# Beside L0's pass of a graph network kernel: part of the source order made by TensorE, edge rows in ten buffers, L3's score steps spread

## The chip, the cores and the metric

One core of one Trainium2 chip runs the whole program. The metric is the device time in microseconds, the median of several runs.

## What is computed

The reference chains four layers on 3125 nodes of 256 features and 50000 edges (`src`, `dst`, sorted by `dst` at the input but with padding and windows handled in the kernel):

```python
x = x + _L0_gnn_ref(_layernorm(x), edge_index, ...)   # sum over edges of h[src]*norm, by dst
x = x + _L0_ffn_ref(...)                              # shared expert and 2 of 8 experts
x = x + _L1_gnn_ref(_layernorm(x), edge_index, edge_attr_256, ...)  # relu(x[src] + edge_attr), by dst
x = x + _L1_ffn_ref(...)                              # 1 of 32 experts
x = x + _L2_gnn_ref(_layernorm(x), src, dst, ...)     # attention, softmax over edges of one src
x = x + _L2_ffn_ref(...)
x = x + _L3_gnn_ref(_layernorm(x), src, dst, ...)     # 4 heads, softmax over edges of one dst
x = x + _L3_ffn_ref(...)
```

The first, third and seventh line need the edges in the order of their target, the fifth also in the order of their source. The third needs the 50000 rows of `edge_attr_256` in the order of the targets.

## The kernel before, in words

The nodes are 25 tiles of 125 rows. Edges in order fill 415 tiles of 128 (`NTE`), none of which crosses a tile of nodes. Each of five engines runs its own program (VectorE `v`, ScalarE `a`, TensorE `p`, GpSimd `g`, SyncE `s`), stages are divided by `K.meet`, at which all five wait for one another, and inside a stage semaphores with counts (`mark`, `ring`) order the work. In the profile the engines are DVE, ACT, PE, POOL and SP.

**The sort** (`Sort`, L514 to L833) gives every edge a slot in the target order. Of the 391 columns of 128 edges, 56 are scattered by GpSimd through DRAM (`recd`, L831); the other 335 are moved by TensorE: VectorE makes a one-hot of the slot's row (L677) and one of its column (L680), ScalarE scales the first with the two halves of a 20-bit code (L795), and two products add them up in PSUM (L751). Meanwhile `EdgeRows` (L928 to L1026) starts to put the rows of `edge_attr` in order: SyncE loads 128 rows (L1008) into one of 5 buffers, GpSimd scatters them to the DRAM table `eaS` (L996), which frees the buffer. There are 391 such scatters, handed out in fixed numbers: 97 in the sort (`EDGES`, L518), 22 after L0's gathers, 2 and 3 (3 and 3 in odd steps) for each of the 25 steps of the stage with the shared expert (`fused_gpsimd`, L1482), and 2 or 3 for each of 54 expert tiles (`expert_gpsimd`, L1632). SyncE's loads are handed out in step with these.

**L0's pass** (`EdgeSum`, L1068 to L1141): for each of the 415 tiles GpSimd gathers 128 rows of `tabA` into a ring of 8 (L1086), VectorE makes a one-hot (L1105), TensorE multiplies (L1138, two instructions for one f32 product), and VectorE adds the result to the accumulator three steps later (L1117). `SourceSort` works beside it by steps of VectorE's loop: windows, picks (steps 30 to 54), scans (60 to 84), placing (120 to 169), and at step 180 the rows of the source order (`rowS`). `L0Out` (L1144) follows without a meet.

**The source order** is made by `SourceScatter` (L904): all 391 columns scattered into `recs` by GpSimd (L920), 2 for each of 54 expert tiles of the first mixture m0, 79 in `L1Mlp`, 2 for each of 25 steps of the scores of the second mixture m1, 19 in its grouping, 1 for each of its 54 expert tiles, and 3 for each of 25 steps of `L2Project` with 6 more after its loop. At its last tile of nodes SyncE waits for the scatters to land (L926), loads `recs`, and VectorE unpacks it behind its loop (L2358 to L2364).

**L3Sum** (L3192 to L3336) is a loop over the 415 edge tiles. TensorE picks scores for tile i-1 (L3322), and multiplies tile i-18 (L3331); VectorE makes the place one-hots of 8 tiles at once (`flip`, L3223), turns the picks of 8 tiles into scores in seven small steps in a row (L3263 to L3277, one group of 8 at a time), ScalarE takes their exponential (L3305), GpSimd weights the rows (L3244), and VectorE adds each product to the accumulator (L3284), each addition waiting for the one before it:

```python
            if i >= self.LAG + 2:
                k = i - self.LAG - 2
                rows = pr.acc[0:PT, bass.ds(at.at(k), AW)]
                v.wait_ge(*self.summed.n(k + 1))
                if k:
                    v.wait_ge(*self.added.n(k))
                v.tensor_tensor(rows, rows, K.bank[4 + k % 4][0:PT, 0:AW], ALU.add).then_inc(*self.added.up)
```

Of the kernel before, what the change touches and what calls it, by code (L numbers as in the profile page):

```python
# [17 lines left out]
N = 3125  # L18
D = 256
T = 25  # L20
# [62 lines left out]
class Kit:  # L83


    def __init__(self, nc, ctx, a, out):
# [23 lines left out]
        self.eidD = sb("eidD", [128, EP], I32)  # L110
        self.locD = sb("locD", [128, EP])
        self.idxS = sb("idxS", [128, EP], I32)
        self.locS = sb("locS", [128, EP])
        self.pkS = sb("pkS", [128, EC], I32)
        self.rowS = sb("rowS", [128, EC], I32)
        self.rowE = sb("rowE", [128, EC], I32)
# [4 lines left out]
        self.wiS = sb("wiS", [128, EP], I32)  # L121
        self.eaB = sb("eaB", [128, D])
# [391 lines left out]
class Sort:  # L514
# [6 lines left out]
    EDGES = 97  # L521
# [313 lines left out]
class SourceSort:  # L835


    def __init__(self, K, sort):
# [4 lines left out]
        self.of = K.W(EC)  # L843

# [6 lines left out]
    def vector(self, v, step):  # L851
# [40 lines left out]
        if step == 197:  # L892
            r.tile_windows(v, K.wtS).then_inc(*own.up)

    def tensor(self, p, step):
# [4 lines left out]
        if step == 193:  # L900
            self.rank.count_starts(p)


class SourceScatter:  # L904


    def __init__(self, K, sort):
        self.K, self.sort = K, sort
        self.sent = K.ring(4, EC, "gather", keep=True)
        self.done = 0  # L910

    def gpsimd(self, g, count):
        K = self.K
        if self.done == 0 and count:
            g.wait_ge(*self.sort.rows.n(1))
            g.wait_ge(*self.sort.ini_s.n(1))
        for c in range(self.done, min(self.done + count, EC)):
            if c >= 4:
                g.wait_ge(*self.sent.n(c - 4))
            g.indirect_dma_start(out=K.recs, out_offset=bass.IndirectOffsetOnAxis(ap=K.rowS[:, c:c + 1], axis=0),  # L920
                                 in_=K.pkS[:, c:c + 1], in_offset=None).then_inc(*self.sent.up(c))
            self.done = c + 1

    def landed(self, eng):
        for c in range(EC - 4, EC):
            eng.wait_ge(*self.sent.n(c))  # L926


class EdgeRows:
# [3 lines left out]
    NB = 5  # L933
    REST = 128 * EP

    def __init__(self, K, sort):
        self.K, self.sort = K, sort
        self.buf = [K.idxS[:, 0:D].bitcast(F32), K.locS[:, 0:D], K.wiS[:, 0:D].bitcast(F32), K.eaB[:, :], K.eidD[:, 0:D].bitcast(F32)]
# [126 lines left out]
class EdgeSum:  # L1065
# [31 lines left out]
    def vector(self, v):  # L1097
        K, acc = self.K, self.acc
        at = Offsets(K, ENG.DVE, K.wiD, 24 * 256)
        for i in range(1, NTE + self.LAG):  # L1100
# [17 lines left out]
            if self.beside:  # L1118
                self.beside.vector(v, i)
        v.wait_ge(*self.added.all)  # L1120

    def scalar(self, a):
        if self.edge_rows:
# [48 lines left out]
class Moe:  # L1172
# [289 lines left out]
    def fused_sync(self, s):  # L1462
# [7 lines left out]
        for t in range(T):  # L1470
# [6 lines left out]
            self.side.edges.sync(s, 6 if t % 2 else 5)  # L1477

    def fused_gpsimd(self, g):
        for t in range(T):  # L1480
# [5 lines left out]
            self.side.edges.gpsimd(g, 3 if t % 2 else 2)  # L1486
# [145 lines left out]
    def expert_gpsimd(self, g):  # L1632
        K = self.K
        for k in range(self.NT):
# [5 lines left out]
            if self.shared and k >= 2:  # L1640
# [3 lines left out]
                self.side.edges.gpsimd(g, k % 2)  # L1644
                self.side.source.gpsimd(g, 2)
# [604 lines left out]
class L2Project(Project):  # L2250
# [4 lines left out]
    def __init__(self, K, source):  # L2255
# [13 lines left out]
        self.raw, self.lo = W(EP, I32), W(EP, I32)  # L2269
        self.ptF = self.acc[:, 0:self.RT * DL]  # L2270
# [25 lines left out]
    def gpsimd(self, g):  # L2296
# [4 lines left out]
        self.source.gpsimd(g, EC)  # L2301

    def sync(self, s):
# [4 lines left out]
        for i in range(T + 3):  # L2308
# [7 lines left out]
            if i == T - 1:  # L2316
# [7 lines left out]
    def vector(self, v):  # L2324
# [33 lines left out]
        v.wait_ge(*self.got.n(1))  # L2358
        v.tensor_scalar(K.idxS[:, :], self.raw, 7, None, ALU.logical_shift_right)
# [832 lines left out]
class L3Sum:  # L3192


    GB, RO, RG, BUFS, LAG = 8, 24, 28, 4, 18
# [778 lines left out]
```

## Time and profile before

| | us |
|---|---|
| median of 3 runs | 5655.34 (5644.27 to 5657.37) |
| the profiled execution | 5645.28 |
| its span | 5643.2 |
| mean granted TensorE clock | 0.834 |

The profile is one execution, traced by the hardware; its span runs from the first instruction to the last. All times are in microseconds from the span's start, means of one instruction in ns. A bracket behind a row gives how long the engine sat idle before it and what ended that. A group's row ends with the idle time before its instructions. A granted clock (PEclk) of 1.00 is 2.4 GHz, one of 0.50 is 1.2 GHz; values between are mixtures over the window.

The stages that matter here lie at: sort 0 to 320, L0's pass 320 to 855, L0Out to 884, shared expert to 1089 and its meet to 1114, m0's experts to 1530, L1's pass from 1600 to 2150, L1Mlp to 2324, m1's scores to 2369 and their meet to 2391, m1's experts to 2600, L2Project 2645 to 2769, L3Sum 4985 to 5358.

### The profile page before, as it was taken

Reading aid. Unit: us, or ns where it says so; the run is one execution under the profiler, and the core shown is the slowest. Engines: PE = TensorE matmul, PEld = TensorE weight load, DVE = VectorE, ACT = ScalarE, POOL = GpSimd, SP = SyncE. Lnnn points to the kernel's source line nnn. Section 1 sums busy time; section 2 is a strip of 40 time slices with the busy share of each in tenths; the row PEclk is TensorE's granted clock in tenths of the full one; section 3 lists DMA queues with packets and bytes.
Section 4 is the critical chain, followed back from the end, with each engine's and each line's share of the span. In section 5 each row is a group of like instructions: output and inputs, shape, how many; then the busy total and the mean of one; then the engine's idle time right before and its main releaser. Section 6 shows DMA issues by size and latency. Waiting matters only on the chain. (4 is left out here: it accounts for less than half of the span.)

```text
span 5643.2 us, 86482 instructions
## 1 busy us (share of the span) xinstructions
PE 4436.4 (79%) x19744; PEld 2874.0 (51%) x19744; DVE 3377.0 (60%) x11730; ACT 2141.2 (38%) x7496; POOL 3551.8 (63%) x3818
## 2 busy tenths in 40 slices
PE   6968887799966778478599968888695788877768
PEld 4423336699823335344355546666593433345536
DVE  8957544310167774534455558887416688867775
ACT  7900002233333334112555545554243455544331
POOL 7777775677567773674777757775124477756620
PEclk8966658899957668555899989999696899999978
DMA  2543346688667771132344458886473588866500
GB/s 62 164 153 103 106 103 190 225 276 275 201 183 206 206 207 38 54 92 75 104 130 130 131 131 286 285 283 197 143 212 99 169 230 231 231 186 190 155 19 23
DMA packets 535499, 914.79 MB, mean 162 GB/s; under 512 B 103029, under 2 KB 385604, under 8 KB 526564
## 3 DMA queue, kind: packets, MB, share of 16 engines
q0 software_dynamic: 161600, 449.89, 28.5%
q1 hardware_dynamic: 312974, 330.74, 18.7%
q10 hardware_dynamic: 60438, 128.64, 7.4%
q8 instruction: 187, 3.06, 0.2%
q14 instruction: 300, 2.46, 0.1%
HBM read 739.18 MB, written 169.72 MB: 161 GB/s over the span
## 5 line engine op out<-in xcount | busy, mean ns | idle before, releaser
L1138 PE MATMUL bank<-small 128*125 128x256 f32 x1660 | 815.3, 611 | 298.6 <-DVE small L1105 175.4
L1086 POOL DMA_INDIRECT small<-tabA,idxD x830 | 801.6, 966 | 263.9 <-issue 189.5
L1138 PEld LDWEIGHTS bank<-small 128*125 128x125 f32 x1660 | 371.6, 276 | 741.6 <-DVE small L1105 401.3
L920 POOL DMA_INDIRECT recs<-pkS,rowS x391 | 385.6, 986 | 226.1 <-issue 100.7
L3085 POOL DMA_INDIRECT small<-tabC,idxD x415 | 410.6, 989 | 185.5 <-DVEq L204 59.4
L2823 POOL DMA_INDIRECT big<-tabB,idxD x415 | 399.4, 962 | 161.9 <-issue 90.5
L1117 DVE TENSOR_TENSOR big<-big,bank 125x256 f32 x830 | 346.4, 417 | 241.6 <-PE bank L1138 230.3
L2549 POOL DMA_INDIRECT big<-tabT,idxS x415 | 404.9, 976 | 136.4 <-issue 104.8
L1671 DVE COPY small<-bank 128x256 f32<-128x256 f32 x176 | 74.7, 425 | 679.4 <-PE bank L1726 679.4
L3163 PE MATMUL bank<-big,cst 128*125 128x512 f32 x830 | 426.1, 594 | 0.5 <-ACT big L3150 0.5
L1715 PE MATMUL bank<-small,big 128*128 128x128 f32 (+1 forms) x3040 | 399.2, 288 | 0.0
L1726 PE MATMUL bank<-big 128*128 (+1 forms) x1520 | 390.9, 404 | 2.4 <-issue 2.4
L1715 PEld LDWEIGHTS bank<-small,big 128*128 128x128 f32 (+1 forms) x3040 | 367.0, 195 | 19.3 <-issue 19.2
L3149 ACT ACTIVATE big<-cst,small 128x128 f32<-128x128 f32 x830 | 286.8, 393 | 235.3 <-DMA small<-tabC,idxD 233.5
L1639 POOL DMA_INDIRECT small<-tabA,small x176 | 169.0, 960 | 310.5 <-PE bank L1702 161.1
L3244 POOL TENSOR_TENSOR big<-big 128x256 f32<-128x256 f32 x415 | 245.5, 630 | 142.2 <-ACT big L3305 142.2
L3331 PE MATMUL bank<-big,small 128*125 128x260 f32 x830 | 268.4, 424 | 63.4 <-DVE big L3284 56.9
L1127 ACT ACTIVATE small<-small 128x256 f32<-128x256 f32 x415 | 172.8, 416 | 370.3 <-DVE small L1110 370.3
L1755 ACT ACTIVATE big<-bank,small 128x128 f32<-128x128 f32 (+1 forms) x760 | 220.7, 367 | 244.0 <-PE bank L1715 240.7
L1726 PEld LDWEIGHTS bank<-big 128*128 128x128 f32 (+1 forms) x1520 | 286.8, 199 | 51.4 <-issue 20.9
L2569 DVE SCALAR_TENSOR_TENSOR small<-bank,big 128x256 f32<-128x256 f32 x415 | 163.1, 421 | 220.2 <-PE bank L2647 219.8
L3132 DVE TENSOR_REDUCE small<-bank 125x4 f32<-125x512 f32 x415 | 282.2, 680 | 0.0
(521 smaller groups left out, 10439.8 us busy)
## 6 DMA issues: line engine op xcount, KB each, us to landing
big<-in_L_w ACTq DMA_DIRECT2D x56, 1024.0 KB
small<-eaS SPq DMA_DIRECT2D x415, 128.0 KB
eaS<-small SPq DMA_DIRECT2D x415, 128.0 KB, 3.8
big<-eaS SPq DMA_DIRECT2D x415, 128.0 KB, 2.8
big<-in_L2f_w ACTq DMA_DIRECT2D x64, 512.0 KB
big<-rowsD SPq DMA_DIRECT2D x104, 256.0 KB, 3.9
ytab<-small ACTq DMA_DIRECT2D x176, 128.0 KB
big<-rowsS SPq DMA_DIRECT2D x52, 256.0 KB
```

The costliest lines, as they stand in the source:

```text
L920: g.indirect_dma_start(out=K.recs, out_offset=bass.IndirectOffsetOnAxis(ap=K.rowS[:, c:c + 1], axis=0), in_=K.pkS[:, c:c + 1], in_offset=N ...
L1086: g.indirect_dma_start(out=self.gb[k % self.RG], out_offset=None, in_=K.tabA, in_offset=row_index(K.idxD, k)).then_inc(*self.got.up(k))
L1117: v.tensor_tensor(rows, rows, K.bank[k % 4][0:PT, 0:D], ALU.add).then_inc(*self.added.up)
L1138: p.matmul(self.K.bank[k % 4][0:PT, 0:D], self.oh[k % self.RO][:, 0:PT], self.gb[k % self.RG], start=True, stop=True).then_inc(*self.summe ...
L1715: m = p.matmul(self.hidden(k, hf)[0:hc, j * 128:j * 128 + 128], w1[:, c * F + f * 128:c * F + f * 128 + hc], xT[:, c, :], start=(c == 0), ...
L1726: m = p.matmul(K.bank[6 + k % 2][:, 0:D], self.hT[k % self.RT][0:hc, f * 128:(f + 1) * 128], K.big[0:hc, bass.ds(where + f * D, D)], start ...
L2549: g.indirect_dma_start(out=self.rows(k)[:, 0, :], out_offset=None, in_=K.tabT, in_offset=row_index(K.idxS, k)).then_inc(*self.got.up(k))
L2823: g.indirect_dma_start(out=self.gb[k % self.RB], out_offset=None, in_=K.tabB, in_offset=row_index(K.idxD, k)).then_inc(*self.got.up(k))
L3085: g.indirect_dma_start(out=self.gb[k % self.RG], out_offset=None, in_=K.tabC, in_offset=row_index(K.idxD, k)).then_inc(*self.got.up(k))
L3132: v.tensor_reduce(self.tm[k % 4][0:PT, 0:4], K.bank[k % L][0:PT, :].rearrange("p (h e) -> p h e", h=4), AXX, ALU.max).then_inc(*self.top.up)
L3149: a.activation(self.diagonals(k, h, 1), K.ident, ACT.Copy, scale=gb[:, D + h:D + h + 1])
L3163: p.matmul(b, K.ones[:, 0:PT], self.dg[k % self.RD], start=False, stop=True).then_inc(*self.field.up)
```

## The change

- The 10 edge buffers are one tensor `edge` (`NB = 10`); `idxS` and `locS` are views of it. Of the 391 edge scatters 80 (not 97) are in the sort, 28 (not 22) behind L0's gathers, 5 in each of the 25 shared-expert steps (not 5 or 6), 3 for each expert tile (not 2 or 3); SyncE's loads follow the same numbers.
- In the last 224 steps of L0's pass (191 to 414) a new class moves the first 224 source columns with TensorE as the sort does: two one-hots by VectorE, two scalings by ScalarE, two products by TensorE into banks 4 and 5. `total` folds them into `sumS` before L0Out (two VectorE operations), and L2Project adds `sumS` to `recs` (two more).
- GpSimd scatters only the other 167 source columns: 1 for each m0 expert tile (54), 79 in L1Mlp as before, 34 beside m1's experts, none in m1's scores and grouping, none in L2Project. `recs` is loaded at L2Project's third tile, not at its last.
- In L3Sum the seven score steps of a group go one at a time between additions, the exponential follows at a fixed step, and products lag by 24 tiles, not 18; `flip` and the place rows are asked for earlier or later to fit.

```diff
-    EDGES = 97
+    EDGES = 80
...
+class SourceMoves:
+    FIRST, N = 191, 224
+    RH, RP, RT = 4, 6, 6
...
+    def vector(self, v, step):
...
+        e = step - self.FIRST
+        if 0 <= e < self.N:
+            if e >= self.RH:
+                v.wait_ge(*self.scaled.n(e - self.RH + 1))
+            v.tensor_scalar(self.here[e % self.RH], self.iota16[:, 0:128], r.pf[:, e:e + 1], None, ALU.is_equal).then_inc(*self.here_v.up)
+            if e >= self.RT:
+                v.wait_ge(*self.placed.n(e - self.RT + 1))
+            v.tensor_scalar(self.ptile[e % self.RT], self.iota16, r.kk[:, e:e + 1], None, ALU.is_equal).then_inc(*self.place.up)
+
+    def scalar(self, a):
+        for e in range(self.N):
+            a.wait_ge(*self.here_v.n(e + 1))
+            if e >= self.RP:
+                a.wait_ge(*self.placed.n(e - self.RP + 1))
+            for b in range(2):
+                ins = a.activation(self.pl[e % self.RP][b], self.here[e % self.RH], ACT.Copy, scale=self.half[b][:, e:e + 1])
+            ins.then_inc(*self.scaled.up)
+
+    def tensor(self, p, k):
+        K, e = self.K, k - self.FIRST
+        if 0 <= e < self.N:
+            p.wait_ge(*self.place.n(e + 1))
+            p.wait_ge(*self.scaled.n(e + 1))
+            for b in range(2):
+                m = p.matmul(K.bank[4 + b][:, 0:EP], self.pl[e % self.RP][b], self.ptile[e % self.RT], start=(e == 0), stop=(e == self.N - 1))
+            m.then_inc(*self.placed.up)
...
-    NB = 5
+    NB = 10
...
-            self.side.edges.sync(s, 6 if t % 2 else 5)
+            self.side.edges.sync(s, 5)
...
-            self.side.edges.gpsimd(g, 3 if t % 2 else 2)
+            self.side.edges.gpsimd(g, 2)
...
-                self.side.edges.gpsimd(g, k % 2)
-                self.side.source.gpsimd(g, 2)
+                self.side.edges.gpsimd(g, 1)
+                self.side.source.gpsimd(g, 1)
...
-        self.source.gpsimd(g, EC)
+        assert self.source.done == EC
...
-            if i == T - 1:
+            if i == 2:
                 self.source.landed(s)
...
+        v.tensor_copy(self.rawf, self.raw).then_inc(*own.up)
+        v.wait_ge(*own.all)
+        v.tensor_tensor(self.raw, self.rawf, K.sumS[:, :], ALU.add).then_inc(*own.up)
...
-    GB, RO, RG, BUFS, LAG = 8, 24, 28, 4, 18
+    GB, RO, RG, BUFS, LAG, SCORE, EXP = 8, 30, 28, 4, 24, 11, 19
...
+            gi, r = divmod(i - self.SCORE, GB)
+            if 0 <= gi < self.n_g and r < 7:
+                self.score_step(v, gi, r)
...
-                 side=SideWork(edges, (0, 3, 0), source, (0, 2, 0)))
+                 side=SideWork(edges, (0, 3, 0), source, (0, 1, 0)))
...
-                 side=SideWork(None, None, source, (2, 1, 19)))
+                 side=SideWork(None, None, source, (0, 1, 0)))
...
-            edges.gpsimd(g, 22)
+            edges.gpsimd(g, 28)
```

`score_step(v, gi, r)` is the old block cut at its waits: r = 0 copies the picks out of PSUM, 1 and 2 add the two other parts, 3 to 6 form the score. `flip` moves from steps 0 to steps 2 of 8, so that its step has no score step.

## Rows read from the trace of the kernel before

**Rows 1.** Windows, core 0: us, busy of PE, PEld, DVE, ACT, POOL, PEclk, DMA share, GB/s

```profile
322.00:843.00 521.00, 421.73 (x823) 191.72 (x823) 316.18 (x952) 0.00 (x0) 395.38 (x412) 0.60 0.38 109
1160.00:1200.00 40.00, 40.00 (x277) 37.41 (x276) 6.46 (x30) 13.70 (x46) 30.33 (x32) 1.00 0.84 274
5014.00:5334.00 320.00, 246.13 (x1468) 173.62 (x1467) 237.64 (x735) 136.10 (x781) 217.31 (x368) 1.00 0.63 189
124.00:292.00 168.00, 159.40 (x804) 79.32 (x804) 166.18 (x764) 162.00 (x540) 131.86 (x117) 1.00 0.49 155
117.30:120.30 3.00, 2.94 (x9) 1.24 (x10) 2.96 (x16) 2.86 (x10) 2.18 (x2) 0.50 0.02 0
```

**Rows 2.** Timeline: VectorE's first work in L0's pass, GpSimd's last edge scatter before it

```profile
319.80 0.87 DVE L1105 TENSOR_SCALAR small<-cst,locD 128x125 f32<-128x125 f32 x3 [27.21 <-ACTq L204]
...
320.95 0.96 POOL L996 DMA_INDIRECT eaS<-locS,rowE  x1 [0.30 <-issue]
```

**Rows 3.** Groups of GpSimd, L0's pass, 600 to 840: busy, mean ns, idle before

```profile
L1086 POOL DMA_INDIRECT small<-tabA,idxD x193 | 182.5, 946 | 58.8 <-issue 47.2 <-PE bank L1138 11.6
```

**Rows 4.** Who VectorE waited for, shared expert's end: us, times, longest

```profile
DVE small L1663 <- issue: 25.4, 1, 25.4
```

**Rows 5.** Who VectorE waited for, m1's scores, then L2Project's end

```profile
DVE small L1398 <- SPq L202: 22.6, 1, 22.6
...
DVE idxS L2359 <- DMA big<-recs: 12.1, 1, 12.1
```

**Rows 6.** Groups of L3Sum, 5014 to 5334 us

```profile
L3284 DVE TENSOR_TENSOR big<-big,bank 125x260 f32 x367 | 155.4, 423 | 73.1 <-PE bank L3331 51.6 <-DVE big L3284 21.4
...
L3244 POOL TENSOR_TENSOR big<-big 128x256 f32<-128x256 f32 x368 | 218.3, 631 | 102.7 <-ACT big L3305 102.7
```

**Rows 7.** Groups of VectorE: the sort's one-hots (120 to 292), L0's addition (600 to 840)

```profile
L680 DVE TENSOR_SCALAR small<-big 128x416 f16<-128x416 f16 x328 | 104.0, 317 | 0.1
L677 DVE TENSOR_SCALAR small<-big 128x128 f16<-128x128 f16 x246 | 61.1, 248 | 0.0
...
L1117 DVE TENSOR_TENSOR big<-big,bank 125x256 f32 x191 | 80.5, 422 | 119.0 <-PE bank L1138 118.1
```

**Rows 8.** Timeline of TensorE: products back to back, one alone, moves at both clocks

```profile
343.74 5.90 PE L1138 MATMUL bank<-small 128*125 128x256 f32 x14
...
836.94 1.19 PE L1138 MATMUL bank<-small 128*125 128x256 f32 x2 [0.21 <-issue]
...
117.36 4.07 PE L751 MATMUL bank<-small 128*128 128x416 f16 x14 [0.88 <-ACT small L795]
...
139.87 1.68 PE L751 MATMUL bank<-small 128*128 128x416 f16 x8
```

**Rows 9.** Groups of GpSimd beside picks (362:392), scans (400:432), moves (185:290)

```profile
L1086 POOL DMA_INDIRECT small<-tabA,idxD x25 | 23.6, 946 | 7.6 <-issue 7.0 <-PE bank L1138 0.6
...
L1086 POOL DMA_INDIRECT small<-tabA,idxD x23 | 25.0, 1088 | 7.0 <-PE bank L1138 4.6 <-issue 2.4
...
L996 POOL DMA_INDIRECT eaS<-idxS,rowE x15 | 17.2, 1150 | 5.0 <-issue 4.3 <-DMA idxS<-in_ea 0.8
```

**Rows 10.** Timeline of GpSimd and VectorE, end of L0's pass and L0Out

```profile
856.15 1.20 POOL L996 DMA_INDIRECT eaS<-wiS,rowE  x1 [3.24 <-DMA wiS<-in_ea]
878.81 0.96 POOL L996 DMA_INDIRECT eaS<-eaB,rowE  x1 [0.30 <-issue]
...
883.26 0.30 DVE L1168 BATCH_NORM_AGGREGATE mv<-st 125x2 f32<-125x6 f32 x2
```

**Rows 11.** Timeline of VectorE inside L3Sum: score steps, additions, a flip

```profile
5101.65 0.22 DVE L3263 COPY small<-bank 128x64 f32<-128x64 f32 x1
5103.27 0.42 DVE L3284 TENSOR_TENSOR big<-big,bank 125x260 f32 x1
5103.89 0.42 DVE L3284 TENSOR_TENSOR big<-big,bank 125x260 f32 x1 [0.20 <-DVE big L3284]
5106.73 0.67 DVE L3223 TENSOR_SCALAR big<-big,lane 128x1024 bf16<-128x1024 bf16 x1
```

More of the change, by code:

```diff
@@ L893, in vector @@
             r.tile_windows(v, K.wtS).then_inc(*own.up)
+        self.moved.vector(v, step)
     def tensor(self, p, step):
@@ L908, in __init__ @@
         self.K, self.sort = K, sort
-        self.sent = K.ring(4, EC, "gather", keep=True)
-        self.done = 0
+        self.first = SourceMoves.N
+        self.sent = K.ring(4, EC - self.first, "gather", keep=True)
+        self.done = self.first
     def gpsimd(self, g, count):
         K = self.K
-        if self.done == 0 and count:
+        if self.done == self.first and count:
             g.wait_ge(*self.sort.rows.n(1))
@@ L917, in gpsimd @@
         for c in range(self.done, min(self.done + count, EC)):
-            if c >= 4:
-                g.wait_ge(*self.sent.n(c - 4))
+            n = c - self.first
+            if n >= 4:
+                g.wait_ge(*self.sent.n(n - 4))
             g.indirect_dma_start(out=K.recs, out_offset=bass.IndirectOffsetOnAxis(ap=K.rowS[:, c:c + 1], axis=0),
-                                 in_=K.pkS[:, c:c + 1], in_offset=None).then_inc(*self.sent.up(c))
+                                 in_=K.pkS[:, c:c + 1], in_offset=None).then_inc(*self.sent.up(n))
             self.done = c + 1
     def landed(self, eng):
-        for c in range(EC - 4, EC):
-            eng.wait_ge(*self.sent.n(c))
+        for n in range(EC - self.first - 4, EC - self.first):
+            eng.wait_ge(*self.sent.n(n))
 class EdgeRows:
-    NB = 5
+    NB = 10
     REST = 128 * EP
@@ L937, in __init__ @@
         self.K, self.sort = K, sort
-        self.buf = [K.idxS[:, 0:D].bitcast(F32), K.locS[:, 0:D], K.wiS[:, 0:D].bitcast(F32), K.eaB[:, :], K.eidD[:, 0:D].bitcast(F32)]
+        self.buf = [K.edge[:, i * D:(i + 1) * D] for i in range(self.NB)]
         self.rowE = K.rowE
@@ L1119, in vector @@
                 self.beside.vector(v, i)
+        if self.beside:
+            self.beside.moved.total(v)
         v.wait_ge(*self.added.all)
     def scalar(self, a):
+        if self.beside:
+            self.beside.scalar(a)
         if self.edge_rows:
@@ L2358, in vector @@
         v.wait_ge(*self.got.n(1))
+        v.wait_ge(*own.all)
+        v.tensor_copy(self.rawf, self.raw).then_inc(*own.up)
+        v.wait_ge(*own.all)
+        v.tensor_tensor(self.raw, self.rawf, K.sumS[:, :], ALU.add).then_inc(*own.up)
+        v.wait_ge(*own.all)
         v.tensor_scalar(K.idxS[:, :], self.raw, 7, None, ALU.logical_shift_right)
@@ L3226, in sync @@
         K = self.K
-        for q in range(3):
+        for q in range(4):
             self.places(s, q)
@@ L3232, in sync @@
             s.dma_start(self.gb[k % self.RG][:, 0:D], K.eaS[k * 128:(k + 1) * 128, :]).then_inc(*self.got.up(k))
-            if k >= 16 and k % 8 == 0 and k // 8 + 1 < self.n_g:
-                self.places(s, k // 8 + 1)
+            if k >= 8 and k % 8 == 0 and k // 8 + 3 < self.n_g:
+                self.places(s, k // 8 + 3)
     def inside(self, k):
@@ L3754, in _ @@
             K.meet(a, "a")
+            l0_sum.scalar(a)
             K.meet(a, "a")
@@ L3856, in _ @@
             edges.sync_last(s)
-            edges.sync(s, 5)
+            edges.sync(s, edges.NB)
             sort.sync_tables(s, edges)
@@ L3861, in _ @@
             l0_sum.sync(s)
-            edges.sync(s, 22)
+            edges.sync(s, 28)
             K.meet(s, "s")
```

105 lines of the change are left out of this document (70 added, 35 removed).

## The prediction

> **What bounds the kernel now.** I read the windows by stage first, then for each stage that the change touches what VectorE waited for at its end, and last the timelines inside the loops. No engine bounds the whole: each stage has its own limit, and an edit pays only where it shortens what ends a stage. The rows to look for are long waits at a meet, for there one engine holds four.
>
> The sort ends with such a wait. VectorE sat 27.2 us idle until 319.8, and GpSimd's last edge scatter is recorded at 320.95, each scatter taking 0.96 busy and 0.30 idle [rows 2] (GpSimd's records run a little behind its queue, so the meet precedes the last of them). L0's pass is paced by GpSimd's gathers: 0.946 + 0.305 = 1.25 us each, almost all the idle time "issue" [rows 3]; TensorE is busy for 422 of 521 us at a mean granted clock of 0.60, which leaves room in it [rows 1]. The shared expert's stage ends with VectorE waiting 25.4 us [rows 4] and GpSimd scattering all the while; m1's scores end with 22.6 us, L2Project with 12.1 us for `recs` [rows 5]. m0's experts are bound by TensorE: 40.00 of 40 us at full clock [rows 1]. In L3Sum VectorE has 51.6 us of waits for TensorE in 320, and TensorE itself is busy for 246 of 320 [rows 6, 1]: neither is full, because the seven score steps stand in a row in VectorE's queue.
>
> **The change part by part.**
>
> *Sort.* 17 scatters fewer before the meet, at 0.96 + 0.30 = 1.265 us: 21.5 us less. VectorE was done at 319.8 - 27.2 = 292.6 and the new meet would be at 298.3, so GpSimd still ends the stage and all 21.5 count: **-21.5**. At most 27.2 could be had; at least some 15, if the ten first loads crowd the stage.
>
> *Moves in L0's pass*, 224 steps. VectorE gets two one-hots, 0.317 + 0.248 us, beside an addition of 0.42 and a one-hot of about 0.3 [rows 7]: together 1.29 of busy time that overlaps at its edges, and less than 1.25 in pitch since the sort does one whole move in 176 us / 335 = 0.53 us with these same operations. ScalarE was idle here [rows 1] and has two scalings. TensorE: seven products back to back took 5.90 us, 0.84 each, at half clock; the pair of a move took 4.07 / 7 = 0.58, over a stretch that was at half clock for its first 3 us, and at full clock 1.68 / 4 = 0.42 at most [rows 8, 1]. At half clock a step wants about 0.84 + 0.69 = 1.53 (0.69 from twice 416 columns at 1.2 GHz), over the 1.25 of the gather; but then TensorE is always busy, and where it was so, 95%, with such moves (124 to 292) the clock was 1.00 throughout, as it was in L3Sum at 77% busy [rows 1]. At full clock the step wants about 0.42 + 0.42 = 0.84, and the gather stays the pace. What is left is what the new VectorE operations do to GpSimd. Beside 25 picks, 391 wide f16 comparisons, one per gather, a gather took 946 ns, as ever; beside the scans 1088; beside the sort's moves, a 416 wide comparison every 0.53 us, a scatter took 1150 [rows 9]. Bounds: nothing, and 0.19 x 224 = 43. The picks are the nearest row (same kind, same density), so I take little: **+5**.
>
> The Trainium skill (SBUF — State Buffer, Who interferes with whom) says that a comparison of this kind can take the port pair it shares with GpSimd, that the loser blocks until the instruction ends, and that this starves the descriptors of GpSimd's DMAs. The picks' 946 ns do not show it, the scans and moves may. It speaks against this change; as a mechanism of this kernel it is rival 2.
>
> *Between pass and shared expert.* `total` adds two VectorE operations on PSUM with their waits, about 1.3, to an L0Out that ended at 883.6. GpSimd has 28 scatters instead of 22: it ended at 879.8, with a stall of 3.2 for a load that ten full buffers avoid; 879.8 - 3.2 + 6 x 1.4 = 885.0 [rows 10]. Both end 1.5 later: **+1.5**.
>
> *Shared expert.* 125 scatters for 137, 12 x 1.27 = 15 us less, and the five loads of a step no longer wait for buffers. GpSimd needs 5 x 1.27 = 6.3 us per step of 198 / 25 = 7.9, so it should keep up and VectorE or TensorE end the stage. The whole wait is 25.4 [rows 4]; I take **-22**, bounds -15 and -25.4. Late next: the first gathers of m0's experts, unchanged.
>
> *m0's experts.* GpSimd issues 1 gather + 3 edges + 1 source per tile, 5 x 1.27 = 6.3 us, where it had 5.5 and 7.0; TensorE needs 40 / (277 / 50) = 7.2, at 50 instructions a tile, and covers it. Half an edge row more per tile is more traffic on DMA engines at 0.84 share [rows 1]; if the weights come late, that cover is gone. **+1**, bounds 0 and +8.
>
> *m1's scores.* GpSimd's 50 scatters (63 us) leave a stage whose other engines were done 22.6 us before the meet [rows 5]: **-22**. The 19 scatters of the grouping were hidden. L1Mlp is unchanged.
>
> *L2Project.* With no scatter to land, `recs` is there before the loop ends: -12.1 [rows 5], and +1.1 for the two added operations on 416 columns: **-11**. The loop itself waited for ScalarE and VectorE, not for GpSimd.
>
> *L3Sum.* A group of 8 tiles takes 320 / 367 x 8 = 6.98 us. From the first score step to the next addition VectorE spends 5103.27 - 5101.65 = 1.62, after 0.34 of the addition before; two additions with nothing between them stand 0.62 apart, since the second waits for the first (0.42 + 0.20) [rows 11]. A score step of about 0.2 fits into that gap. So a group loses 1.62 + 0.34 - 0.62 = 1.34, and gets 0.17 back at the flip, where now a step stands ahead of 0.5 to 0.67 [rows 11]: 1.17 x 52 = 61 less. The lag of 24 for 18 costs six short fill steps, 2 us. New pace 5.8 us per group; GpSimd needs 8 x 0.6 = 4.8 and TensorE 8 x 246 / 367 = 5.4 [rows 6, 1], so both are close but under it. **-59**, bounds -30 (TensorE or a hand-off takes over) and -80 (pace of TensorE, 5.4).
>
> *Sum*: -21.5 + 5 + 1.5 - 22 + 1 - 22 - 11 - 59 = **-128**. The profiled execution took 5645.3, 10 under the median of the three shown; from the median, 5655.3 - 128 = 5527.
>
> **The rivals.**
>
> 1. *Forecast*, 5527.
> 2. *GpSimd's gathers are slowed by VectorE's f16 one-hots.* For: scans and sort moves, +0.14 to +0.2 a piece [rows 9]. Against: the picks. 0.19 x 224 = 43, less the 5 counted: 5565.
> 3. *L3Sum finds another bound*: TensorE or the in-order queues, with a gain of 15 to 20 only. For: TensorE 77% busy with register loads in its stream. Against: additions 0.62 apart run in long rows. 5527 + 42 = 5569.
> 4. *TensorE falls behind in part of the moves*: at half clock 1.53 - 1.25 = 0.28, x 224 = 63: 5590.
> 5. *The other side: TensorE takes over L0's step.* It stays at half clock, and as it waits in order for one-hots, gather and scaled one-hots, nothing runs back to back: a product alone takes 1.19 [rows 8], then 0.15 to the next piece and 0.69 for the pair, 2.03 a step. (2.03 - 1.25) x 224 = +175 beside the other terms' -133: 5697, slower by 0.7%. It decides from 1.84 a step on. For: a mean clock of 0.60 in this pass. Against: the clock of 1.00 beside the sort's moves.
> 6. *More than forecast*: L3Sum at TensorE's pace, the whole 25.4 gained, no slowing of gathers: 5500.
> 7. *Not what it says*: late source data would have to be waited for elsewhere; the 167 scatters end in m1's experts, two stages ahead of their use, so this has nothing for it.
>
> **How the numbers follow.** Chances: forecast 0.58, 2: 0.13, 3: 0.11, 4: 0.06, 5: 0.04, 6: 0.08. 2 and 3 together would be 5607. The likeliest gives 5527. The range 5490 to 5592 takes in 6, 2, 3 and 4, with the bounds of the shared-expert and sort terms inside; 5 and pairs of rivals stay out. A measurement of this kernel tells about 0.3%, 17 us, from no change. Every case but 5 and double failures gives over 17 us: faster 0.93, same 0.03, slower 0.04.
>
> **What would show it.** Right: VectorE's idle time before L0's pass near 6 us and none over 5 at the shared expert's and m1's meets; gathers of L0's second half at a pitch of 1.25 to 1.30 with PEclk near 1.00 from step 191 on; in L2Project no wait for `recs`; L3Sum 310 to 316 us long instead of 373, additions 0.62 apart with one score step between. Wrong: gather pitch over 1.4; POOL waiting for PE in the pass; PEclk staying at 0.5 there; PE idle for weights in m0's experts; a group of L3Sum over 6.5 us.

## The result, and the profile after

The changed kernel takes 5519.4 us (5517.6 to 5524.2, 4 runs) against 5653.8 (5644.3 to 5657.4, 4 runs): a ratio of 0.9765, 95% interval 0.9752 to 0.9778, or 134 us less. 5527 was predicted, with a range of 5490 to 5592.

| | before | after |
|---|---|---|
| median | 5653.8 | 5519.4 |
| profiled execution, its span | 5645.28, 5643.2 | 5524.19, 5522.4 |
| mean granted TensorE clock | 0.834 | 0.853 |

The profiled executions differ by 121 us, not 134. Both traces can be laid beside each other instruction by instruction, as nearly every line exists in both; the table says by how much each stage became longer or shorter (the first or last instruction of a line in one trace against the same one in the other).

| stage | predicted | measured |
|---|---|---|
| sort, to L0's first addition | -21.5 | -23.7 |
| L0's pass, with 224 moves | +5 | +2.2 |
| `total` and what follows | +1.5 | +1.1 |
| shared expert with its meet | -22 | -22.6 |
| m0's experts | +1 | -2.7 |
| m1's scores with their meet | -22 | -22.5 |
| m1's experts | 0 | +1.7 |
| L2Project with `recs` | -11 | -11.1 |
| L2's combination loop (not changed) | 0 | +18.1 |
| L3Sum | -59 | -63.0 |
| all the rest | 0 | +1.7 |
| sum | -128 | -120.8 |

Without the loop that nobody had changed the stages add up to -139. A row of this table compares one execution with one, and the start of L0's pass alone moves by some us between executions (next paragraph).

**Sort** (the rows after to [rows 2]). The timeline of VectorE and GpSimd, then the same addition in the kernel before:

```profile
294.24 0.75 DVE L1175 TENSOR_SCALAR small<-cst,locD 128x125 f32<-128x125 f32 x3 [1.94 <-SPq L200]
306.14 0.42 DVE L1187 TENSOR_TENSOR big<-big,bank 125x256 f32 x1 [11.15 <-PE bank L1212]
...
297.80 0.96 POOL L1066 DMA_INDIRECT eaS<-edge,rowE  x1 [0.31 <-issue]
299.06 0.99 POOL L1156 DMA_INDIRECT small<-tabA,idxD  x1 [0.30 <-issue]
```

```profile
329.88 0.42 DVE L1117 TENSOR_TENSOR big<-big,bank 125x256 f32 x1 [9.20 <-PE bank L1138]
```

VectorE's wait at the meet is 1.9 us, not the 6 that were foretold, and yet the stage gained only 23.7. GpSimd's records run behind its queue: the meet opened at 294.2, while the last scatter is recorded at 297.80, and the rest of the wait moved behind the meet, to the first addition (11.15 for 9.20). The pair "wait at the meet, wait behind it" is to be read together. GpSimd's scatters run without a gap into its first gather, but the engine that VectorE's row names at the meet is now SyncE (`SPq`): the two end the stage close together.

Both numbers belong to this execution. Seven profiles below have this same sort (after twice, flip_gap, half_products, recs_late, short_weight, twice_onehot): VectorE waits 1.4 to 8.4 us at the meet, each time for SyncE, and the first addition starts at 305.1 to 311.0 us, at 308.2 in the mean. In the four profiles with the old sort it starts at 329.9 to 331.2, at 330.4 in the mean. Over all of them the sort gained 22 us.

**L0's pass and the other loops** (after to [rows 1]; windows: us, busy of PE, PEld, DVE, ACT, POOL, PEclk, DMA share, GB/s), and two groups of the pass between 560 and 800 (after to [rows 3, 7]):

```profile
560.00:800.00 240.00, 189.12 (x766) 94.70 (x767) 204.87 (x768) 132.76 (x383) 181.79 (x192) 1.00 0.37 106
4960.00:5220.00 260.00, 234.34 (x1467) 168.75 (x1467) 231.98 (x731) 140.94 (x780) 211.63 (x366) 1.00 0.77 229
1100.00:1140.00 40.00, 40.00 (x278) 37.41 (x277) 6.78 (x30) 13.74 (x46) 30.44 (x32) 1.00 0.95 310
```

```profile
L1156 POOL DMA_INDIRECT small<-tabA,idxD x192 | 182.4, 950 | 58.5 <-PE bank L1212 48.8 <-issue 9.7
...
L943 DVE TENSOR_SCALAR small<-small,big 128x416 f16<-128x416 f16 x192 | 65.6, 342 | 0.0
```

240 / 192 = 1.25 us per gather, 950 ns each: GpSimd still sets the pace and isn't held up. TensorE runs at full clock in the pass, where it had 0.60.

**The waits that should go** (after to [rows 4, 5]): what VectorE waited for behind the shared expert (us, times, longest), then its timeline across the meet behind m1's scores.

```profile
DVE small L1737 <- issue: 1.7, 2, 1.4
```

```profile
2322.86 0.18 DVE L1411 FIND_INDEX8 small<-small 125x8 uint32<-125x32 f32 x1
2323.18 0.18 DVE L1472 CAST small<-small 125x25 f32<-125x25 uint32 x1
```

25.4 us became 1.7. L1472 is the line that waited 22.6 us for the meet (L1398 before) and now follows the last index 0.14 us after its end; for `recs` VectorE doesn't wait at all any more (no such wait in 2640 to 2700).

**L3Sum** (after to [rows 6, 11]): groups of 4960 to 5220, then VectorE's timeline from a score step to a flip.

```profile
L3339 DVE TENSOR_TENSOR big<-big,bank 125x260 f32 x366 | 155.0, 423 | 28.0 <-DVE big L3339 8.7 <-PE bank L3422 3.1 <-issue 1.4
L3303 DVE TENSOR_SCALAR big<-big,lane 128x1024 bf16<-128x1024 bf16 x45 | 30.5, 677 | 0.0
L3367 DVE TENSOR_TENSOR small<-big,small 128x32 f32<-128x32 f32 x46 | 17.5, 380 | 0.0
L3370 DVE SCALAR_TENSOR_TENSOR small<-small 128x32 f32<-128x32 f32 x45 | 13.0, 289 | 0.0
L3373 DVE TENSOR_TENSOR small<-small 128x32 f32<-128x32 f32 x45 | 11.1, 246 | 0.0
...
L3359 DVE TENSOR_TENSOR small<-small,bank 128x64 f32<-128x64 f32 x46 | 9.8, 213 | 0.0
```

```profile
5050.21 0.42 DVE L3339 TENSOR_TENSOR big<-big,bank 125x260 f32 x1
5050.55 0.18 DVE L3373 TENSOR_TENSOR small<-small 128x32 f32<-128x32 f32 x1
5050.84 0.42 DVE L3339 TENSOR_TENSOR big<-big,bank 125x260 f32 x1
5051.18 0.17 DVE L3376 TENSOR_SCALAR small<-small 128x32 f32<-128x32 f32 x1
5051.26 0.48 DVE L3303 TENSOR_SCALAR big<-big,lane 128x1024 bf16<-128x1024 bf16 x1
5051.66 0.42 DVE L3339 TENSOR_TENSOR big<-big,bank 125x260 f32 x1
5052.28 0.43 DVE L3339 TENSOR_TENSOR big<-big,bank 125x260 f32 x1 [0.20 <-DVE big L3339]
```

Additions stand 0.63 apart (5050.21, 5050.84) with a step between them; only the flip stretches a gap, to 0.82. A group of 8 takes 260 / 366 x 8 = 5.68 us, where 5.8 was forecast, and VectorE's waits for TensorE fell from 51.6 us of 320 to 3.1 of 260. What was not foreseen: the three operations from L3367 on took 191 to 192 ns before and take 380, 289 and 246 now, and the flip 677 for 625. Those that read PSUM (L3359) did not become slower (213 for 220).

### The profile page after: what moved, and what is told of

It is laid out like the page before. It is cut to its first block and busy times, and to the rows that moved or that the text cites. A ratio compares the mean times of both kernels' runs of the same rounds, so it can differ in the third digit from the quotient of the medians.

```text
span 5522.4 us, 88485 instructions
## 1 busy us (share of the span) xinstructions
PE 4435.7 (80%) x20192; PEld 2884.0 (52%) x20192; DVE 3479.8 (63%) x12187; ACT 2302.5 (42%) x7944; POOL 3326.5 (60%) x3594
## 5 line engine op out<-in xcount | busy, mean ns | idle before, releaser
L1212 PE MATMUL bank<-small 128*125 128x256 f32 x1660 | 733.8, 555 | 286.9 <-DVE small L1175 172.2
L1212 PEld LDWEIGHTS bank<-small 128*125 128x125 f32 x1660 | 336.4, 251 | 680.7 <-issue 361.8
L2629 POOL DMA_INDIRECT big<-tabT,edge x415 | 404.0, 973 | 247.8 <-SPq L200 121.6
L1066 POOL DMA_INDIRECT eaS<-edge,rowE x391 | 393.0, 1005 | 164.7 <-issue 114.3
L951 ACT ACTIVATE small<-small,big 128x128 f16<-128x128 f16 x448 | 155.3, 394 | 385.3 <-DVE small L940 384.2
L2492 PE MATMUL bank<-big,small 125*128 x1245 | 217.1, 283 | 87.7 <-DVE small L2932 35.5
```

What stands on the lines that cost most here:

```text
L1066: g.indirect_dma_start(out=K.eaS, out_offset=bass.IndirectOffsetOnAxis(ap=self.rowE[:, c:c + 1], axis=0), in_=self.buf[c % self.NB], in_of ...
L1212: p.matmul(self.K.bank[k % 4][0:PT, 0:D], self.oh[k % self.RO][:, 0:PT], self.gb[k % self.RG], start=True, stop=True).then_inc(*self.summe ...
L2629: g.indirect_dma_start(out=self.rows(k)[:, 0, :], out_offset=None, in_=K.tabT, in_offset=row_index(K.idxS, k)).then_inc(*self.got.up(k))
```

## The experiments

Twelve kernels. For L3Sum "the loop" is the time from its first to its last addition (L3284, L3339 after) in the trace: 358.4 us before and 295.4 after. How far it moves by itself: nine profiles with after's L3Sum and a full weighting, the flip where after has it (after twice, edges76, five_buffers, half_products, l3sum_only, old_spread, recs_late, twice_onehot) have 293.3 to 297.2, 295.7 in the mean.

**1. L3Sum alone.** The class `L3Sum` of after in the kernel before; its diff is that of the change.

> The kernel before, with L3Sum of the kernel after and nothing else of the change. Theory (the parts are independent, each stage is paid for where its own end lies): the stages up to L2Project stay as they were and L3Sum's loop takes about 295 us instead of 358, so 5653.8 - 63 = 5591 us, ratio 0.989. Rival (the earlier stages' gains let later ones start in another state, or L3Sum gained only because GpSimd and the DMA engines had less left to do): L3Sum stays over 320 us, 5615 or more.

Measured: 5593.9 us, ratio 0.9887 (0.9863 to 0.9912), loop 295.6. The theory holds: L3Sum gains the same without the rest of the change, and this half is worth 0.0113 x 5655 = 64 us.

**2. The lag alone.**

```diff
-    GB, RO, RG, BUFS, LAG = 8, 24, 28, 4, 18
+    GB, RO, RG, BUFS, LAG = 8, 30, 28, 4, 24
```

> The kernel before, with only LAG 24 instead of 18 and RO 30 instead of 24 in L3Sum; the seven score steps still stand in a row. Theory (the gain comes from spreading the score steps, for the block costs VectorE 1.3 us per group of 8 in its own queue): the loop stays within 5 us of 358 plus the six extra fill steps, 5650 to 5658 us. Rival (the deeper lag is what hides the block's latency and brings most of the gain): the loop falls by 20 to 60 us, 5595 to 5635.

Measured: 5775.8 us, ratio 1.0208 (1.0182 to 1.0234), loop 470. Neither the theory nor the rival. VectorE's waits in L3Sum:

```profile
DVE big L3223 <- DMA big<-rowsD: 95.0, 41, 3.8
```

The place rows of a group were requested behind the load of row tile k, and that load waits for the product of tile k - 28: with a lag of 24 it comes six steps later, and the flip, which is due at a fixed step, stands ahead of the additions in VectorE's queue. The edit of SyncE's order in the change, to which the prediction gave no price, repairs this: it takes 97 of the 112 us away (experiment 3). Beside the 95 us of waits the granted clock was lower, too: at half for 174 us of this loop, for 5 in the kernel before.

**3. The lag with its row schedule.**

```diff
-    GB, RO, RG, BUFS, LAG = 8, 24, 28, 4, 18
+    GB, RO, RG, BUFS, LAG = 8, 30, 28, 4, 24
...
-        for q in range(3):
+        for q in range(4):
...
-            if k >= 16 and k % 8 == 0 and k // 8 + 1 < self.n_g:
-                self.places(s, k // 8 + 1)
+            if k >= 8 and k % 8 == 0 and k // 8 + 3 < self.n_g:
+                self.places(s, k // 8 + 3)
```

> The kernel before, with LAG 24 and RO 30 as in the run before this one and now also the place rows asked for as the change asks for them (four ahead, then row group k // 8 + 3 behind load k); the seven score steps still stand in a row. In the run before, VectorE waited 95 us for those rows. Theory (spreading the score steps is what gains; the lag alone gains next to nothing, and its row schedule only repairs what the lag breaks): L3Sum's loop 350 to 362 us, 5647 to 5660 us. Rival (lag and rows are most of the gain, the block in a row hardly matters once the pipeline is deep): the loop 300 to 320 us, 5595 to 5615.

Measured: 5672.0 us, ratio 1.0026 (1.0015 to 1.0037), loop 373.8. The rows no longer wait, but the loop is 15 us longer than before. A group and a window (5030 to 5330):

```profile
L3331 PE MATMUL bank<-big,small 128*125 128x260 f32 x653 | 240.5, 477 | 53.7 <-POOL big L3244 48.6 <-DVE big L3284 4.0
```

```profile
5030.00:5330.00 300.00, 244.93 (x1305) 173.33 (x1305) 213.64 (x653) 122.54 (x690) 190.26 (x327) 0.87 0.61 179
```

TensorE now waits for GpSimd's weighted rows where it waited for VectorE's additions, but it doesn't wait longer: over the whole loop it sat idle for 68 us, and for 80 in the kernel before. What grew is its own work, 306 us busy for 278, at a granted clock of 0.88 for 0.99: in this loop the clock fell to half 21 times, for 92 us together; before it fell once, for 5 us. A product took 473 ns for 423. It is not one bad execution: the mean clock of the whole program was 0.819 to 0.828 in all eight runs of this kernel, and 0.826 to 0.834 in the eleven of before beside them.

The rival is refuted, and the theory was too mild. With the score steps in a row the deeper lag costs 15 us, and they come through the clock, which neither the prediction nor the expectation had considered. With that lag the rest of the new L3Sum is worth 78 us (373.8 to 295.4), the lost clock included (3.5 us at half clock in after). Lag and rows alone gain nothing, so the 63 us need the spread steps; spread steps at the old lag of 18 were not run, nor the spreading without the moved exponential and flip.

**4. The flip in the empty gap.** After's L3Sum, `flip` behind the addition of its step.

```diff
-            if i < NTE and i % 8 == 2 and i // 8 + 1 < self.n_g:
-                self.flip(v, i // 8 + 1)
...
                 v.tensor_tensor(rows, rows, K.bank[4 + k % 4][0:PT, 0:AW], ALU.add).then_inc(*self.added.up)
+            if i < NTE and i % 8 == 2 and i // 8 + 1 < self.n_g:
+                self.flip(v, i // 8 + 1)
```

> The kernel after, with L3Sum's place comparison (flip) issued behind the addition of its step instead of ahead of it, so that it falls into the one gap of eight that has no score step; now the last score step and the flip stand in the same gap. Theory (VectorE's chain of additions, 0.62 us a piece plus what does not fit into the gaps, sets the pace): about 0.2 us less per group, 52 groups, 8 to 11 us less: 5510. Rival (TensorE, 90% busy in this loop, sets the pace): nothing, 5519.

Measured: 5521.4 us, ratio 0.9769 (0.9743 to 0.9796), loop 299.9. Nothing gained, the theory falls. The flip itself became cheaper (565 ns for 677) and L3367 dearer (476 for 380); VectorE's waits for its own additions fell from 9.7 to 0.8 us in the loop, and its waits for TensorE rose from 12.7 to 28.0 (its groups and waits, 4940 to 5200):

```profile
L3303 DVE TENSOR_SCALAR big<-big,lane 128x1024 bf16<-128x1024 bf16 x44 | 24.8, 565 | 0.1
L3367 DVE TENSOR_TENSOR small<-big,small 128x32 f32<-128x32 f32 x44 | 20.9, 476 | 0.0
```

```profile
DVE big L3337 <- PE bank L3422: 17.2, 26, 0.9
```

**5. The kernel after once more.**

> The kernel after, unchanged, beside the others: 5519 us. Its profile is a second look at the L2 combination loop, which took 550 us in the first profile of this kernel against 532 before, with eleven short drops of the granted clock against one. Theory (these drops come and go from one execution to the next, with no link to the change): another length of this loop and another number of drops. Rival (the change causes them): again about 550 us and some ten drops.

Measured: 5519.0 us, ratio 0.9758 (0.973 to 0.9786); L2's combination loop 535.4 us with three drops of the clock inside it (nine of the eleven of the first profile lie inside it). The theory holds, and every other profile here adds a sample of that loop, whose code is the same in all 14; seven of them:

| length, us | of it at half clock, us | kernel |
|---|---|---|
| 531.6 | 6.1 | before |
| 533.0 | 6.6 | flip_gap |
| 535.4 | 12.4 | after_again |
| 540.7 | 25.3 | l3lag_rows |
| 545.1 | 29.9 | l3sum_only |
| 547.3 | 41.7 | edges76 |
| 549.7 | 47.4 | after |

The profile of before had the shortest and that of after the longest of the fourteen, and the more of the loop was at half clock, the longer it took. The same 100 us of it, in the first and in the second profile of after (window's columns as above):

```profile
3595.00:3695.00 100.00, 86.08 (x570) 65.87 (x568) 81.61 (x369) 49.85 (x145) 69.55 (x73) 0.91 0.85 264
```

```profile
3595.00:3695.00 100.00, 87.25 (x625) 68.38 (x624) 87.49 (x402) 54.34 (x157) 74.81 (x78) 1.00 0.89 284
```

So 18 us of the difference between the two profiles belong to the executions, and the -120.8 has to be read as some -139 by the stages; the medians give -134.

**6. A short weighting.** What makes VectorE's small operations slow in the new L3Sum?

```diff
-            rows = self.gb[k % self.RG][:, 0:D].rearrange("p (h c) -> p h c", h=4)
+            rows = self.gb[k % self.RG][:, 0:D].rearrange("p (h c) -> p h c", h=4)[:, :, 0:8]
...
-            g.tensor_tensor(rows, rows, self.pr.EX[:, 4 * k:4 * k + 4].unsqueeze(2).broadcast_to([128, 4, 64]), ALU.mult).then_inc(*self.weighted.up)
+            g.tensor_tensor(rows, rows, self.pr.EX[:, 4 * k:4 * k + 4].unsqueeze(2).broadcast_to([128, 4, 8]), ALU.mult).then_inc(*self.weighted.up)
```

> The kernel after, with GpSimd's weighting of a tile in L3Sum cut to 8 of 64 columns of each head (so 7 of 8 parts of the messages stay unweighted); everything else stays. It tells what the small VectorE score steps, 364 to 380, 281 to 289 and 246 to 249 ns now against 191 to 192 before, wait for. Theory (an operation of VectorE whose operands all lie in SBUF waits while GpSimd works, one that reads PSUM does not): the three fall back to about 190 ns and the flip from 670 to under 600, and the loop, 293 to 295 us, gets about 0.5 us per group shorter at most, 265 to 290. Rival A (they are slow from their own semaphore traffic): they stay at 380, 289 and 249. Rival B for the pace (TensorE alone sets it): the small ones fall, the loop stays at 290 or more.

Measured: 5503.7 us in one run, loop 289.5.

```profile
L3324 POOL TENSOR_TENSOR big<-big 128x32 f32<-128x32 f32 x376 | 75.8, 240 | 185.5 <-ACT big L3396 185.5
L3303 DVE TENSOR_SCALAR big<-big,lane 128x1024 bf16<-128x1024 bf16 x45 | 21.8, 484 | 0.0
...
L3367 DVE TENSOR_TENSOR small<-big,small 128x32 f32<-128x32 f32 x47 | 10.2, 218 | 0.0
...
L3373 DVE TENSOR_TENSOR small<-small 128x32 f32<-128x32 f32 x47 | 8.8, 186 | 0.0
L3370 DVE SCALAR_TENSOR_TENSOR small<-small 128x32 f32<-128x32 f32 x47 | 8.7, 186 | 0.0
```

With GpSimd at 76 us of 260 for 212, 380, 289 and 246 ns fall to 218, 186 and 186, and the flip from 677 to 484. GpSimd's work was what they waited for; rival A is refuted. The loop gained only 4 to 6 us against after's two profiles (295.4, 293.3), 6 against the mean of the nine: TensorE was busy for 238 of 260 us here. 289.5 lies at the very end of the theory's 265 to 290 and next to rival B's 290 or more: nearly all of the pace is TensorE's.

**7. A second comparison in each move.**

```diff
+            v.tensor_scalar(self.spare[e % 3], self.iota16[:, 0:384], r.kk[:, e:e + 1], None, ALU.is_equal)
             v.tensor_scalar(self.ptile[e % self.RT], self.iota16, r.kk[:, e:e + 1], None, ALU.is_equal).then_inc(*self.place.up)
```

> The kernel after, with one more f16 comparison of 384 columns by VectorE in each of the 224 move steps, into a tile that nobody reads. VectorE, 205 of 240 us busy in this stretch, would need about 1.35 us a step and become the pace of the loop: 224 x 0.1 to 0.15 = 20 to 35 us longer. What it is to tell is the gathers' own time. Theory (f16 comparisons of this kind do not hold up GpSimd's gathers, however dense): 945 to 965 ns each as now. Rival (the sort's scatters took 1150 beside moves because VectorE was 99% busy with such operations; a full VectorE holds GpSimd up): 1050 to 1150 ns.

Measured: 5517.6 us in one run; L0's pass ends 0.4 us later than after's.

```profile
560.00:800.00 240.00, 193.25 (x768) 95.88 (x767) 239.63 (x961) 133.18 (x384) 181.51 (x193) 0.99 0.37 106
```

```profile
L1158 POOL DMA_INDIRECT small<-tabA,idxD x193 | 182.7, 947 | 58.8 <-PE bank L1214 49.7 <-issue 9.1
```

VectorE is busy for 239.6 of 240 us and the gathers take 947 ns. For the gathers the theory holds even beside a full VectorE; the 20 to 35 us were wrong, since VectorE's operations overlap: the five of a step, 1.85 us by their own durations, fit into 1.25.

**8. Half the products.**

```diff
+            n = 16 if e % 2 and e < self.N - 1 else EP
-                m = p.matmul(K.bank[4 + b][:, 0:EP], self.pl[e % self.RP][b], self.ptile[e % self.RT], start=(e == 0), stop=(e == self.N - 1))
+                m = p.matmul(K.bank[4 + b][:, 0:n], self.pl[e % self.RP][b], self.ptile[e % self.RT][:, 0:n], start=(e == 0), stop=(e == self.N - 1))
```

> The kernel after, with the two products of every second move cut from 416 to 16 columns (so a part of the source order is left out). It tells what the granted clock of this stretch hangs on. Theory (TensorE's own busy share lifts it, so the moves made themselves cheaper): the mean granted clock of 560 to 800 falls from 1.00 to between 0.6 and 0.95, and the gathers' pitch stays at 1.25 us. Rival (something else in this stretch gives the full clock, ScalarE's and VectorE's work beside it for one): 1.00 stays, pitch 1.25.

Measured: 5518.9 us in one run; L0's pass took 1 us longer than after's.

```profile
560.00:800.00 240.00, 166.54 (x770) 97.27 (x769) 203.13 (x773) 134.07 (x387) 181.81 (x192) 0.97 0.37 106
```

The clock fell, but only to 0.97, outside the theory's 0.6 to 0.95 and not the rival's 1.00: 14 of the 240 us were at half clock, 0 to 6 in the nine profiles with all products, 172 to 192 in the four without moves. That TensorE's own work lifts it is supported (0.60 without moves, 0.97 with half, 1.00 with all), though not separated from ScalarE's and VectorE's new work, which stayed. Nor was the number of products halved: every second pair still ran, 16 columns wide, at 172 ns a piece.

**9. The old spread of the edge scatters** (97 in the sort, 22 behind L0, 5 or 6 in a shared-expert step), with ten buffers.

```diff
-    EDGES = 80
+    EDGES = 97
...
-            self.side.edges.gpsimd(g, 2)
+            self.side.edges.gpsimd(g, 3 if t % 2 else 2)
...
-            edges.gpsimd(g, 28)
+            edges.gpsimd(g, 22)
```

> The kernel after (ten buffers, source moves, new L3Sum), with the edge scatters before m0's experts handed out as in the kernel before: 97 in the sort (not 80), 22 behind L0's gathers (not 28), 5 or 6 in a shared-expert step (not 5). Theory (each scatter ahead of an end that GpSimd sets costs its own 1.265 us): L0's first addition 17 x 1.265 = 21.5 us later; VectorE and GpSimd end L0 within 2 us of now; m0's experts start another 12 x 1.27 - 1 = 14 to 20 us later: 5519 + 36 to 42 = 5555 to 5561, ratio 0.983. Rival (the gain of the shared expert's stage came from the ten buffers, not from the 12 scatters fewer): sort 21 us, shared expert under 5: 5540 to 5546.

Measured: 5545.0 us, ratio 0.9809 (0.9792 to 0.9825). GpSimd's first gather of L0 comes 21.6 us later (17 scatters at 1.265 are 21.5), L0's first addition 18.8, the end of the pass 21.8, VectorE's start on m0's experts 21.9, the experts' end 27.4. The number is the rival's, 5540 to 5546: with ten buffers the 12 scatters more in the shared expert's stage cost nothing at its meet, where VectorE waits 2.0 us (1.7 in after). They aren't free, though. GpSimd's scatters run without a gap through the meet up to its first gather for the experts, at 1096.64 for 1070.20, 26.4 later, 4.6 more than VectorE's start; TensorE waits 5.4 us more for those gathers (14.2 for 8.8), and that is the rest.

**10. Five buffers**, everything else as in after.

```diff
-    NB = 10
+    NB = 5
```

> The kernel after, with NB = 5 edge buffers. Theory (loads landed in time with five buffers nearly everywhere; the ten only fill one stall behind L0's gathers and some at the shared expert's first steps): sort unchanged within 2 us, 0 to 10 us more up to m0's experts, under 3 in them: 5519 to 5532. Rival (the steady five loads per step need ten buffers to be ahead, with five GpSimd waits for a load in most shared-expert steps): 20 us or more, all of it at the shared expert's meet: 5540 and up.

Measured: 5551.4 us, ratio 0.9823 (0.9805 to 0.9842). L0's pass ends 0.6 us later, m0's experts start 10.7 later and take 28 us more. Neither the theory nor the rival had that. GpSimd's and TensorE's waits there, 1080 to 1510:

```profile
POOL eaS L1066 <- DMA edge<-in_ea: 85.1, 41, 6.0
```

```profile
PE bank L1775 <- DMA small<-tabA,small: 36.6, 6, 20.4
```

In after GpSimd waits 0.6 us for loads in this stage. Three scatters per tile, on DMA engines that are 0.82 full over the stage, need more than five buffers; GpSimd's gathers for the experts stand behind the scatters in its queue, so TensorE, the bound of this stage, runs dry. The longest of its six waits, 20.4 us, is mostly the meet. Of the 28 us, 6 are TensorE's later first product (8 us behind VectorE's start, 2 in after), 12 the other waits (16.2 for 4.1), and 10 more are time in which TensorE was busy, at a granted clock of 0.97 for 0.99; the last part is not followed up here.

**11. `recs` loaded late.**

```diff
-            if i == 2:
+            if i == T - 1:
                 self.source.landed(s)
```

> The kernel after, with recs loaded at the last tile of nodes of L2Project, as before, not at the third. The 12.1 us wait had two causes that the prediction did not separate: the scatters that landed late, and the load itself. Theory (mostly the scatters): VectorE waits 2 to 5 us for recs. Rival (mostly the load, issued late and queued behind the stores of the loop): 8 to 12 us, as before, so that moving the load alone made the 11 us.

Measured: 5522.5 us in one run, and

```profile
DVE big L2435 <- DMA big<-recs: 2.2, 1, 2.2
```

So, by this one run, about 10 of the 12.1 us were the scatters that landed late, and 2 the load's place.

**12. Four scatters fewer in the sort.**

```diff
-    EDGES = 80
+    EDGES = 76
```

> The kernel after, with 76 edge scatters in the sort, not 80; the counts behind still reach 391. In the profile of after GpSimd's last scatter before L0's pass starts at 297.80 while VectorE has its slots at 292.3. Theory (GpSimd still ends the sort): L0's first addition 4 x 1.265 = 5 us earlier and the gain kept to the end, for the last edge rows of m0's experts are covered: 5514, ratio to before 0.975. Rival (the four scatters come back at the end of m0's experts or in L1's pass, whose rows they are): no gain, 5519 or over.

Measured: 5515.3 us, ratio 0.9752 (0.9736 to 0.9768), no difference from after that can be told, and none from the theory's 5514 either. L0's first addition comes 0.6 us later than in the first profile of after, not 5 earlier; but with 80 scatters it starts anywhere from 305.1 to 311.0, and 306.7 here lies inside that.

```profile
290.80 3.20 SPq L1078 DMA_DIRECT2D edge<-in_ea  x3
294.05 0.44 SPq L225 DMA_DIRECT2D tabA<-big  x1
294.54 0.42 SPq L226 DMA_DIRECT2D tabA<-big  x1
```

```profile
297.52 0.99 POOL L1156 DMA_INDIRECT small<-tabA,idxD  x1 [1.00 <-SPq L200]
```

GpSimd now waits for SyncE, as VectorE does at this meet in every profile with ten buffers and 76 or 80 scatters. SyncE issues 3 loads behind each of 24 table stores, 72 after the first ten, whatever `EDGES` says, and the last of them waits for the 72nd scatter to free its buffer; the last table's store stands behind it. The next us at this place is to be looked for in SyncE's queue; how many there are was not measured.

## Why the prediction was right, and where its terms were off

- **The sort**, -21.5, measured -23.7, and -22 over all profiles. The size is right; 17 scatters at 1.265 us each, as experiment 9 shows from the other side (21.6). The reading that GpSimd still ends the stage alone was not: SyncE's queue is the last at the meet, and the wait foretold as 6 us was 1.4 to 8.4, from one execution to the next.
- **The moves**, +5, measured +2.2 by the stages; no kernel without the moves was run. The clock came as argued from the sort's moves, to 1.00, and rivals 4 and 5 fell. Rival 2 fell too: experiment 7 shows no slowing of the gathers even with VectorE 99.8% busy. Taking the picks as the nearest row was right. The Trainium skill (SBUF — State Buffer, Who interferes with whom) would have them starved of descriptors; the trace of experiment 7 doesn't agree, with 947 ns. Why the sort's scatters take 1138 to 1150 ns beside moves stays open.
- **The shared expert**, -22, measured -22.6: right in size, wrong in how it was split. The prediction took 15 from 12 scatters fewer and the rest from the buffers. By experiments 9 and 10 the ten buffers alone bring all of it at the meet and the fewer scatters alone about 12 (22.6 - 10.7). The two causes overlap and may not be added. Beside ten buffers the fewer scatters bring 5 us behind the meet, in the experts' first gathers.
- **m0's experts**, +1, measured -2.7. The bound of +8 held only because of the ten buffers; with five it is +28. The prediction named the cover ("TensorE needs 7.2 us and covers it") but priced GpSimd's instructions, not the loads that they wait for.
- **m1's scores and L2Project**, -22 and -11, measured -22.5 and -11.1. Experiment 11 shows the cause of the second; that of the first is read from the waits before and after, not tested by a run.
- **L3Sum**, -59, measured -63.0. Rival 3 fell. The step of 1.17 us saved per group was (358.4 - 295.4) / 52 = 1.21. The next bound is near, as the term's lower end said: TensorE is 90% busy, and experiments 4 and 6 relieve VectorE and gain 6 us at most. The lag, priced at 2 us, is part of a bundle: alone it costs 15, which come with a lower granted clock, and 112 without the row schedule; in after the start of the stage up to the first addition even became 0.9 us shorter.
- **The sum.** -128 from the terms, -139 by the stages without the disturbed loop, -134 by the medians. Against the stages it was 11 us too timid: 4 in L3Sum, 4 in m0's experts, 3 in the moves, 2 in the sort, less 2 lost in the rest. Against the medians it was 6 too timid in the difference and 8 in the time (5519 for 5527). Two of the terms were right partly by luck: the shared expert's split and the price of the lag were wrong, and nothing came of it because the change made both parts of each together.

## What to carry to other kernels

An engine that holds four others at a meet is worth its whole idle time, but only down to the next queue that waits for the same buffers: read SyncE's queue as well as GpSimd's. Small dependent steps in a row in an in-order queue cost their latency; put one each into the gaps that a chain of dependent operations leaves anyway, and move with them everything that is due at a fixed step. Before a term of a few us is read off two profiles, compare a stage that the change doesn't touch, and look for the same row in every other profile that shares its code; and before a longer loop is put down to the wait that its row names, compare the granted clock and the engine's own busy time.

## What the runs showed of the hardware

- VectorE's operations wait for GpSimd by where their operands lie, as far as these runs tell. Beside GpSimd's f32 product of two SBUF operands, VectorE's with two SBUF inputs (L3367) took 380 ns, and 218 beside a short one, while one with a PSUM input (L3359) stayed at 213; a comparison of 1024 bf16 columns took 677 and 484. Experiment 6 shows that GpSimd's work is the cause. This agrees with the Trainium skill (SBUF — State Buffer, Who interferes with whom), which lets two-input operations and the two-port modes contend with GpSimd.
- GpSimd's gathers don't show it from their side: 946 ns with VectorE 51% busy, 950 at 85%, 947 at 99.8%.
- TensorE's granted clock was 0.60 at 81 to 84% busy with f32 products alone in L0's pass and 0.97 at 69% with half of the f16 moves among them: its busy share in the profile doesn't tell its clock, for at half clock the same work fills more of the time (the same f32 product took 631 ns in the mean without the moves and 412 with them).
- In L2's combination loop, with TensorE 85 to 90% busy, the clock fell to half for moments, up to nine times per execution of the same code; the loop took 18 us longer with 47 us at half clock than with 6.
- The order of the work can bring such drops in every run: in L3Sum a deeper lag with the score steps in a row had 92 us at half clock where the old lag had 5, with TensorE idle for less of the time (68 us for 80).
